# Normalised rows of an attention stage: split in half-precision parts on ScalarE and GpSimd and turned by DMA, in place of TensorE transposes

## What is computed

```python
x = x + 0.5 * ffn(layernorm(x))     # 8 experts, each takes the 2048 rows with the largest gates
x = x + attn(layernorm(x))
x = x + 0.5 * ffn(layernorm(x))
# attn(z): q, k, v = z Wq', z Wk', z Wv'; softmax(causal(q k' / 16)) v Wo'
# ffn first: xn = z * rsqrt(mean(z*z) + eps) * norm_w; logits = xn router' + b; softmax over experts
```

## Time and profile before

| | |
|---|---|
| three runs | 2349.33, 2350.32, 2350.61 us |
| profiled execution | 2350.4 us, span 2348.7 us |
| busy over the span | PE 2008.8 (86%), PEld 1429.0 (61%), ACT 1439.1 (61%), DVE 1427.1 (61%), POOL 1236.4 (53%) |
| DMA transposes | 256, 128 in each mixture of experts |
| attention stage | from 959 to 1516.5 us of the span (SyncE loads its first groups at 959.17) |

### The profile page before, as it was taken

The page is one execution under the profiler, slowest core; times in us unless marked ns, Lnnn a source line. Parts: engine busy times, 40 slices in busy tenths (PEclk is TensorE's granted clock), DMA queues, the critical chain, the costliest instruction groups (busy, mean ns, idle before and its releaser), DMA issues.

```text
span 2348.7 us, 44477 instructions
## 1 busy us (share of the span) xinstructions
PE 2008.8 (86%) x15482; PEld 1429.0 (61%) x15482; DVE 1427.1 (61%) x3912; ACT 1439.1 (61%) x2836; POOL 1236.4 (53%) x1529
## 2 busy tenths in 40 slices
PE   4721799999999999499999999611999999999997
PEld 4621466666666667377777777510666666666665
DVE  6988654544545432389888898697545445445431
ACT  6932566666666665277767777432766666666663
POOL 6701666666666663244343443203666667666763
PEclk9555899999999999799999999855999999999998
DMA  8891465465555542232232322201456456545542
GB/s 283 282 315 36 113 117 99 85 111 98 94 107 99 95 75 40 48 100 97 91 107 80 107 91 87 101 1 49 109 100 116 84 94 120 92 88 115 82 68 32
DMA packets 284102, 241.31 MB, mean 103 GB/s; under 512 B 159792, under 2 KB 263216, under 8 KB 283696
## 3 DMA queue, kind: packets, MB, share of 16 engines
q1 hardware_dynamic: 226608, 172.06, 25.6%
q0 software_dynamic: 57344, 67.29, 19.2%
HBM read 120.76 MB, written 101.71 MB: 95 GB/s over the span
## 4 chain that ended last, share of the span: by engine, by line
PE 80%; DVE 11%; ACT 3%; issue 2%; DMA 1%; POOL 1%; SPq 0%; POOLq 0%; ACTq 0%; DVEq 0%
PE ps L1150 25%; PE ps L1151 24%; PE ps L1152 24%; DVE junk L890 3%; PE ps L1171 2%; PE ps L1253 1%; PE ps L1306 1%; ACT zz L626 1%; DVE nmax L1102 1%; DVE bst L814 1%; PE ps L1266 1%; DVE seen L978 0%; DMA z_d<-zz 0%; DVE pt_l L1081 0%; ACT pr L755 0%
## 5 line engine op out<-in xcount | busy, mean ns | idle before, releaser
L1011 DVE SCALAR_TENSOR_TENSOR hid_l<-hf,hid_h 128x512 f16<-128x512 f32 x512 | 354.9, 694 | 607.7 <-ACT hid_h L600 594.4
L1150 PE MATMUL ps<-w_h,hid_h 128*128 128x256 f16 x2048 | 558.4, 273 | 0.0
L1152 PE MATMUL ps<-w_h,hid_l 128*128 128x256 f16 x2048 | 558.3, 273 | 0.0
L1151 PE MATMUL ps<-w_l,hid_h 128*128 128x256 f16 x2048 | 558.3, 273 | 0.0
L682 ACT ACTIVATE hf<-ps,b 128x512 f32<-128x512 f32 x512 | 348.7, 681 | 134.8 <-PE ps L1152 123.1
L1150 PE MATMUL ps<-xt,w_h 128*128 128x512 f16 x1024 | 390.5, 381 | 35.5 <-DMA xt<-xs 35.5
L1151 PE MATMUL ps<-xt,w_h 128*128 128x512 f16 x1024 | 390.3, 381 | 0.0
L1152 PE MATMUL ps<-xt,w_l 128*128 128x512 f16 x1024 | 390.3, 381 | 0.0
L600 ACT ACTIVATE hid_h<-hf 128x512 f16<-128x512 f32 x512 | 322.4, 630 | 16.2
L600 ACT ACTIVATE ys<-ps,weight 128x256 f32<-128x256 f32 x256 | 121.1, 473 | 343.1 <-PE ps L1152 342.2
L535 POOL DMA_INDIRECT xe<-z_d,row_at x256 | 260.5, 1018 | 101.8 <-issue 77.4
(11 more groups left out here) (241 smaller groups left out, 4047.3 us busy)
## 6 DMA issues: line engine op xcount, KB each, us to landing
w_st<-fc_t SPq DMA_DIRECT2D x32, 1024.0 KB, 5.4
xin<-x SPq DMA_DIRECT2D x32, 512.0 KB, 5.3
z_d<-zz SPq DMA_DIRECT2D x32, 512.0 KB, 4.0
...
xe<-z_d,row_at POOLq DMA_INDIRECT x256
xt<-xs SPq DMA_TRANSPOSE x256
```

The costliest lines, as they stand in the source:

```text
L1011: dve.scalar_tensor_tensor(hid_l[:, n % 2, f, :], hf[:, f % HF, :], HS, hid_h[:, n % 2, f, :], ALU.mult, ALU.subtract).then_inc(s_hl, 1)
L1150: pe.matmul(dst, lh, rh, start=first, stop=False)
L1151: pe.matmul(dst, lh, rl, start=False, stop=False)
L1152: return pe.matmul(dst, ll, rh, start=False, stop=last)
```

## The change

Neither norm is turned by TensorE any more. ScalarE copies the normalised rows to 16 bits (`zr`, and `z2r` for the second norm, 128x1024 each in one instruction), GpSimd subtracts to get the low parts, and SyncE turns high and low parts of each tile with one DMA transpose, four for a group, into `zc` (three buffers) and `z2c` (two). `zt_h`, `zt_l` are no longer written in this stage; the matmuls of u, v, scores and logits read `zc` and `z2c`.

The turn gets deeper: norm (z) one turn after the load, u and v (f) two, scores and values (a) three, second norm (r) four, logits (l) five, at the end of TensorE's turn. The stage has 38 turns instead of 36 and no loop: all are written out. The two halves of u are made at two places of the turn (`u_part`), the split of v is finished by VectorE in the next turn, behind the maxima, and `s_mv2`, `s_scale2` get a second buffer.

```diff
@@ tiles
-        z2t_h = sb("z2t_h", [P, KD, S], F16, att)
-        z2t_l = sb("z2t_l", [P, KD, S], F16, att)
+        zr = sb("zr", [P, TG, 2, D], F16, att)
+        zc = sb("zc", [P, 3, 2, KD, S], F16, att)
+        z2r = sb("z2r", [P, TG, 2, D], F16, att)
+        z2c = sb("z2c", [P, 2, 2, KD, S], F16, att)
...
@@ SyncE
+            def att_turn(c):
+                z, r = c - 1, c - 4
+                if on(c + 2):
+                    x_in(c + 2)
+                if on(z):
+                    sp.wait_ge(s_zrl, z + 1)
+                    wait(sp, s_s, TG * (z - 2))
+                    columns(zc[:, z % 3], zr, s_zc)
+                if on(r):
+                    sp.wait_ge(s_x2, TG * (r + 1))
+                    sp.dma_start(group(outf, r), x2[:, r % 2]).then_inc(s_x2st[r % 2], 16)
+                    sp.wait_ge(s_z2l, r + 1)
+                    wait(sp, s_lg, NG + r - 1)
+                    columns(z2c[:, r % 2], z2r, s_z2c)
+                    sp.dma_start(packed(z_d, r), z2[:, r % 2]).then_inc(s_zst[r % 2], 16)
+
+            x_in(0)
+            x_in(1)
+            for c in range(NG + DEPTH):
+                att_turn(c)
...
@@ GpSimd
-            def att_turn(c, u):
+            def att_turn(c):
+                z, r = c - 1, c - 4
+                if on(r):
+                    pool.wait_ge(s_mv2, r + 1)
+                    wait(pool, s_z2, r - 1)
+                    row_factors(2 + r % 2, 1).then_inc(s_scale2, 1)
+                if on(z):
+                    pool.wait_ge(s_zrh, z + 1)
+                    pool.tensor_tensor(zr[:, :, 1, :], zz[:, z % 2], zr[:, :, 0, :], ALU.subtract).then_inc(s_zrl, 1)
                 if on(c):
                     pool.wait_ge(s_mv, c + (NG // 2 + 1))
-                    pool.wait_ge(s_z, c + NG)
-                    row_factors(0, 1).then_inc(s_scale, 1)
-                a = c - 2
-                if on(a):
-                    pool.wait_ge(s_mv2, a + 1)
-                    wait(pool, s_z2, a)
...
@@ ScalarE
                         if q == 0:
                             wait(act, s_x2, TG * (a - 1))
                         act.activation(pr[:, q, 0:P * (q + 1)], bank(q)[:, 0:P * (q + 1)], ACT.Exp,
-                                       bias=nbias[:, q:q + 1], scale=SCORE, accum_out=rsum[:, u % 2, q:q + 1]).then_inc(s_prob, 1)
+                                       bias=nbias[:, q:q + 1], scale=SCORE, accum_out=rsum[:, a % 2, q:q + 1]).then_inc(s_prob, 1)
+                    pth(a, 0)
+                if on(z):
+                    act.wait_ge(s_scale, z + (NG // 2 + 1))
+                    wait(act, s_zrl, z - 1)
+                    rows(zz[:, z % 2], xin[:, z % WIDE], z % 2, (0, 1))
                 if on(a):
-                    pth(a, 0)
                     pth(a, 1)
+                if on(z):
+                    rows(zz[:, z % 2], xin[:, z % WIDE], z % 2, (2, 3)).then_inc(s_z, 1)
                 if on(f):
-                    wait(act, s_s, TG * (f - 1))
-                    hi_halves(s_tp, f + NG, flat(zt_h[:, (u - 1) % 2]), s_th)
+                    hi_half(s_u, f, u_h, s_uh, 0)
                 if on(a):
                     pth(a, 2)
+                if on(z):
+                    act.wait_ge(s_z, z + (NG + 1))
+                    wait(act, s_zc, 16 * TG * z)
+                    copy(zr[:, :, 0, :], zz[:, z % 2]).then_inc(s_zrh, 1)
+                if on(a):
                     pth(a, 3)
+                if on(f):
+                    hi_half(s_u, f, u_h, s_uh, 1)
                 if on(r):
-                    v = (u - 3) % 2
                     act.wait_ge(s_scale2, r + 1)
-                    act.wait_ge(s_lg, r + (NG - 1))
-                    wait(act, s_zst[v], 16 * (NG // 2) + 8 * (r - v))
-                    normalise(z2[:, v], x2[:, v], 1).then_inc(s_z2, 1)
+                    wait(act, s_zst[r % 2], 16 * (NG // 2) + 16 * (r // 2))
+                    rows(z2[:, r % 2], x2[:, r % 2], 2 + r % 2, range(TG)).then_inc(s_z2, 1)
+                    act.wait_ge(s_z2, r + 1)
+                    wait(act, s_z2c, 16 * TG * r)
+                    copy(z2r[:, :, 0, :], z2[:, r % 2]).then_inc(s_z2h, 1)
                 if on(f):
-                    hi_halves(s_u, f, flat(u_h[:, :, :]), s_uh)
-                if on(r):
-                    hi_halves(s_z2t, r, flat(z2t_h[:, :, :]), s_z2h, 0)
-                if on(f):
-                    hi_halves(s_v, f, flat(v_h[:, :, :]), s_vh)
-                if on(c):
-                    act.wait_ge(s_scale, c + (NG // 2 + 1))
-                    wait(act, s_tp, KD * (c + (NG - 1)))
-                    normalise(zz[:, u % 2], xin[:, u], 0).then_inc(s_z, 1)
-
-            turns(act, att_turn)
+                    hi_half(s_v, f, v_flat_h, s_vh, 0)
+                    hi_half(s_v, f, v_flat_h, s_vh, 1)
+
+            for c in range(NG + DEPTH):
+                att_turn(c)
             stage_end(act, 3)
             route(1)
...
@@ VectorE
+                    group_logits(l - 1, 7, NG)
                 if on(a):
                     ptl(a, 0)
                     ptl(a, 1)
                 if on(f):
-                    lo_halves(s_th, f + NG, flat(zt_l[:, (u - 1) % 2]), flat(zt_h[:, (u - 1) % 2]), s_tl)
+                    lo_half(s_uh, f, u_l, u_h, s_ul, 0)
                 if on(a):
                     residual(a, 0, v, ring)
                     ptl(a, 2)
                     residual(a, 1, v, ring)
                     ptl(a, 3)
                 if on(c):
-                    dve.wait_ge(s_in[u], 16 * (NG // WIDE) + ((c - u) * (16 // RING) + 16))
-                    dve.wait_ge(s_scale, c + NG // 2)
-                    stats(xin[:, u], 0).then_inc(s_mv, 1)
+                    dve.wait_ge(s_in[c % WIDE], 16 * (NG // WIDE + c // WIDE + 1))
+                    wait(dve, s_scale, c + (NG // 2 - 1))
+                    stats(xin[:, c % WIDE], c % 2).then_inc(s_mv, 1)
                 if on(f):
-                    lo_halves(s_uh, f, flat(u_l[:, :, :]), flat(u_h[:, :, :]), s_ul)
-                if on(r):
-                    lo_halves(s_z2h, r, flat(z2t_l[:, :, :]), flat(z2t_h[:, :, :]), s_z2l, 0)
+                    lo_half(s_uh, f, u_l, u_h, s_ul, 1)
                 if on(a):
                     residual(a, 2, v, ring)
                     residual(a, 3, v, ring)
-                if on(a):
                     dve.wait_ge(s_x2, TG * (a + 1))
-                    wait(dve, s_scale2, a)
-                    stats(x2[:, v], 1).then_inc(s_mv2, 1)
-                if on(f):
-                    lo_halves(s_vh, f, flat(v_l[:, :, :]), flat(v_h[:, :, :]), s_vl)
-
-            turns(dve, att_turn, steps)
+                    wait(dve, s_scale2, a - 1)
+                    stats(x2[:, v], 2 + a % 2).then_inc(s_mv2, 1)
+
+            for c in range(NG + DEPTH):
...
@@ TensorE
-            def att_turn(c, u):
-                f, a, r = c - 1, c - 2, c - 3
-                zf = (u - 1) % 2
+            def u_part(f, m):
+                pe.wait_ge(s_zc, 16 * TG * (f + 1))
+                wait(pe, s_vl, KD * (f - 1) + (m + 1))
+                for k in range(KD):
+                    last = split3(ps[2][:, m, :], (g_h[:, k, m * P:(m + 1) * P], g_l[:, k, m * P:(m + 1) * P]),
+                                  (zc[:, f % 3, 0, k, :], zc[:, f % 3, 1, k, :]), k == 0, k == KD - 1)
+                last.then_inc(s_u, 1)
+
+            def v_part(f, h):
+                pe.wait_ge(s_ul, KD * f + (h + 1))
+                for t in (2 * h, 2 * h + 1):
+                    for k in range(KD):
+                        cols = slice(t * P, (t + 1) * P)
+                        last = split3(ps[2][:, h, (t % 2) * D:(t % 2 + 1) * D], (zc[:, f % 3, 0, k, cols], zc[:, f % 3, 1, k, cols]),
+                                      (m_h[:, k, :], m_l[:, k, :]), k == 0, k == KD - 1)
+                last.then_inc(s_v, 1)
+
+            def att_turn(c):
+                f, a, l = c - 2, c - 3, c - 5
                 if on(a):
                     for q in range(TG):
-                        scores(a, u % 2, q)
-                if on(r - 1):
-                    wait(pe, s_ptl, TG * (a - 1) + TG if on(a - 1) else TG * NG)
-                    pe.wait_ge(s_z2l, KD * r)
-                    logit_products(7, z2t_h[:, :, :], z2t_l[:, :, :]).then_inc(s_lg, 1)
+                        scores(a, a % 3, q)
                 if on(a):
                     pt(a, 0)
                 if on(f):
-                    def rear_read(k):
-                        wait(pe, s_vl, KD * (f - 1) + (k + 1))
-                    pe.wait_ge(s_z, f + (NG + 1))
-                    transposes(ps[2], zz[:, zf], s_tp, rear_read)
+                    u_part(f, 0)
                 if on(a):
                     pt(a, 1)
                     values(a, 0)
@@ -1340,31 +1373,21 @@
                     values(a, 1)
                     pt(a, 3)
                 if on(f):
-                    pe.wait_ge(s_tl, KD * (f + (NG + 1)))
```

(52 more changed lines are left out.)

71 lines of the change are left out of this document (36 added, 35 removed).

## The result

The changed kernel takes 2363.71 us, median of four runs (2362.89 to 2364.89), beside 2349.82 for the kernel before (2349.08 to 2350.61): 1.0057 times as long, 95% interval 1.0046 to 1.0069. 2360 was forecast.

The account below looks back on a forecast made before the run. TensorE, 97% busy, bounded the old kernel; after the change, a chain of waits was to hold the turn at 16.28 us. Sum: 2350.4 - 3 (turns) + 6.5 (head) + 6.5 (tail) = 2360.4 us; forecast 2360, own range 2352 to 2366.

Parts of the forecast that it names:

- The chain: Attention turn: hand-overs between VectorE, TensorE and ScalarE from fourth maximum to third values, 7.07 us, then 9.21 of unbroken TensorE work.
- second pair of rows: ScalarE's second pair of first-norm rows, starting at 3.47 us after pt_h and delaying u_h; half of 1.97 us.
- values 3: TensorE's third values, waiting 0.45 us for the third pt_l and starting 7.07 us after the fourth maximum starts.
- the first hand-over: VectorE's v_l half ends at 1.47 us; TensorE hears of it 0.03 later and starts u at 1.50.
- 31 turns: Middle of the attention stage: turns go from 16.34 to 16.28 us, -2 us, taken as -3 for first and last turns.
- Head: Start of attention stage: ScalarE copy 1.14, GpSimd subtraction 2.35 and transposes 6.51 replace 3.45 us; +6.5 us.
- Tail: End of attention stage: last store of z queues behind copy, subtraction and four transposes, +8.7 less about 2.2; +6.5 us.
- TensorE's 1.81 us a turn: TensorE loses 16 transposes a turn, 0.88 + 0.93 us; nearly all returns as three new waits (1.56, 0.4, 0.45).
- Rival 1: Attention turn: chain shorter, only the wait for v_l left, 15.4 us a turn; 2334 us, faster; chance 0.12.
- Rival 2: GpSimd and SyncE become the loop: 17.0 us a turn, 2386 us; SyncE alone +166 at 2.5 a transpose; chance 0.15.
- Rival 3: VectorE's nbias held behind GpSimd's second subtraction: +1.3 us a turn, +40 us, 2400 us; chance 0.10.
- second risk, rinv: VectorE's rinv, if it meets GpSimd's first subtraction, is held: chain up to 2.35 us longer, +73 us at most.

Follow-up runs that it names:

- x1: Changed kernel with VectorE forming both low halves of v behind the second maximum and bias, not the fourth; ratio to the kernel before 0.9946, stage 546.8 us.
- x2: Changed kernel with ScalarE's norm row pairs behind the first and second exponentials, not between copies of transposed probabilities; ratio to the kernel before 0.9968, stage 548.9 us.
- x5: Changed kernel plus one GpSimd subtraction a turn (128x1024, result unused), timed to run beside VectorE's rinv; ratio to the kernel before 1.0241, stage 612.9 us.
- x3: Changed kernel with both edits, those of x1 and x2; ratio to the kernel before 0.9792, stage 508.3 us.
- y2: Changed kernel with each GpSimd subtraction cut in four pieces, each followed by its transpose; ratio to the kernel before 1.0044, stage 563.95 us.
- y1: Changed kernel with one z2 buffer instead of two, so rows wait for the store of the group before; ratio to the kernel before 1.0069, stage 571.2 us.
- y4: Changed kernel with 12 unused TensorE transposes of the identity a turn, ahead of the first probability transpose; ratio to the kernel before 1.0049, stage 566.7 us.
- x4: Changed kernel with each of GpSimd's two subtractions a turn done twice; ratio to the kernel before 1.0102, stage 582.7 us.

## Why the prediction came out as it did

- **The chain set the turn, and its steps are those named.** Predicted and measured, from the start of the fourth maximum at 1238.41: u starts 1.50, 1.62; second pair of rows 3.47, 3.61; u_l starts on VectorE 5.07, 5.21; rinv 5.65, 5.81; third pt_l 6.46, 6.62; values 3 at 7.07, 7.23. The error arises at the first hand-over: v_l's first half ends at 1239.88 and TensorE starts at 1240.03, 0.15 later, where I took 0.03. The rest carries it. x1, x2 and x5 each moved one step and x3 two, and the turn followed.
- **31 turns: -3 predicted, +1.5 measured.** The mis-sized term: 16.28 predicted for a typical turn, 16.45 measured; 28 turns of it, three of 15.83. In the sum the middle was 4.5 us too low and the two ends together 0.9 too high, which leaves the forecast 3.6 us short of the +13.6 of the stage.
- **Head +6.5, measured +6.1.** The parts were 1.14, 2.35 and 6.51; ScalarE took 1.06, GpSimd 2.12, and from the first of the four transposes at 974.90 to TensorE's first matmul at 981.36 passed 6.46:

```profile
971.62 1.06 ACT L612 ACTIVATE zr<-zz 128x1024 f16<-128x1024 f32 x1
...
972.75 2.12 POOL L590 TENSOR_TENSOR zr<-zz,zr 128x1024 f16<-128x1024 f32 x1 [3.33 <-ACT zr L612]
...
974.90 5.12 SPq L423 DMA_TRANSPOSE zc<-zr  x4
...
981.36 0.58 PE L1176 MATMUL ps<-zc,g_h 128*128 128x512 f16 x1 [38.46 <-DMA zc<-zr]
```

- **Tail +6.5, measured +6.0.** y2 confirms that both hang on this trip, y1 that the store of the second norm's rows can stand in the tail's way as well.
- **TensorE's 1.81 us a turn came back as waits**: right, and y4 shows it from the other side for the place of the first eight transposes. It put none where the second eight had stood.
- **Rival 1** (only the wait for v_l left, 15.4): refuted, the waits at the second and third values are there (59 in 30 turns).
- **Rival 2** (GpSimd and SyncE): not here; but I put GpSimd's turn at 13.1 and it is 12.0, since `row_factors` takes 3.9 and not 4.2, and at subtractions of twice the length I had given 17.0 a turn where x4 has 16.7 on average.
- **Rival 3** (nbias held): refuted by its 128 rows, of which 56 ran beside the subtraction. The same paragraph's second risk, rinv, did not arise, by a margin of 0.6 us (rinv ends at 1244.38, its reciprocal at 1244.60, and GpSimd's subtraction starts at 1244.99); x5 made it arise, and it cost 46 us in the stage. I had priced it at 73 at most.
